# Attention steps of 512 and 234 columns instead of two halves of 373, in an audio tower on one core

## What is computed

```python
y = relu(patches @ W.T + b); h = batchnorm(y)                    # (16, 746, 128)
x = layernorm(h); q, k, v = heads(x @ Wq.T + bq), heads(x @ Wk.T + bk), heads(x @ Wv.T + bv)
probs = softmax(q @ k.T * 16 ** -0.5)                            # 8 heads, 746 x 746
h = h + merge(probs @ v) @ Wo.T + bo
x = layernorm(h); e = argmax(x @ Wr + br)                        # one expert a token; its gate is 1
h = h + relu(x @ W1[e] + b1[e]) @ W2[e] + b2[e]
```

## Time and profile before

| | |
|---|---|
| time, median of 3 runs (lowest to highest) | 1233.38 us (1231.71 to 1234.83) |
| span of the profiled execution | 1275.9 us; the profile gives no other time of its own |
| mean granted clock of TensorE | 0.965 |
| PE busy | 1178.7 us (92%) |
| DVE busy | 1072.5 us (84%) |
| ACT busy | 950.6 us (75%) |
| POOL busy | 680.0 us (53%) |
| load of a Q or K part, issue to landing (median) | 2.4 us |

### The profile page before, as it was taken

The page is one execution under the profiler, slowest core; times in us unless marked ns, Lnnn a source line. Parts: engine busy times, 40 slices in busy tenths (PEclk is TensorE's granted clock), DMA queues, the critical chain, the costliest instruction groups (busy, mean ns, idle before and its releaser), DMA issues.

```text
span 1275.9 us, 53879 instructions
## 1 busy us (share of the span) xinstructions
PE 1178.7 (92%) x21379; PEld 745.5 (58%) x21379; DVE 1072.5 (84%) x2756; ACT 950.6 (75%) x2477; POOL 680.0 (53%) x894
## 2 busy tenths in 40 slices
PE   6479999999999999999999999999999846899996
PEld 3334656555555556555555556565644326899996
DVE  7469899999999999999999999999999544577774
ACT  4426988888887878788888878797877824567774
POOL 2062436566473837475665739374723334456664
PEclk9768999999999999999999999999999969899998
DMA  8152132222313131323223131313220513333331
GB/s 190 39 84 79 40 86 72 76 84 61 94 52 94 45 105 42 104 72 79 83 63 93 51 94 45 106 41 104 72 80 28 150 56 105 88 93 105 103 101 50
DMA packets 79409, 102.32 MB, mean 80 GB/s; under 512 B 15916, under 2 KB 72995, under 8 KB 78734
## 3 DMA queue, kind: packets, MB, share of 16 engines
q1 hardware_dynamic: 70624, 79.02, 23.4%
q0 software_dynamic: 8384, 20.22, 5.1%
q10 hardware_dynamic: 186, 0.02, 0.0%
HBM read 60.76 MB, written 38.93 MB: 78 GB/s over the span
## 4 chain that ended last, share of the span: by engine, by line
PE 63%; DVE 20%; issue 5%; POOL 3%; ACT 2%; DMA 1%; SPq 1%; another core or an unknown queue 1%; POOLq 0%; DVEq 0%; ACTq 0%
PE psum L1247 36%; DVE half_max L1112 14%; PE psum L1312 13%; PE psum L1391 6%; PE psum L1401 5%; PE psum L1252 2%; ACT arena L808 2%; DVE stats L916 1%; POOL out_dram L720 1%; DVE rows L990 1%; PE psum L1382 1%; POOL arena L405 1%; DMA arena<-max_rows 1%; PE psum L1267 1%; DVE arena L962 1%
## 5 line engine op out<-in xcount | busy, mean ns | idle before, releaser
L1112 DVE TENSOR_REDUCE half_max<-psum 128x1 f32<-128x373 f32 x1536 | 760.8, 534 | 62.8 <-PE psum L1247 55.0
L808 ACT ACTIVATE arena<-psum 128x373 f32<-128x373 f32 (+1 forms) x1536 | 655.0, 489 | 154.4 <-PE psum L1247 139.0
L1247 PE MATMUL psum<-k_rows,arena 96*32 96x373 bf16 x6144 | 519.1, 329 | 14.9 <-DVE half_max L1112 6.1
L1247 PE MATMUL psum<-arena,k_rows 98*32 98x373 bf16 x6144 | 515.7, 326 | 13.7 <-ACT arena L808 6.2
L1312 PE MATMUL psum<-arena,values 128*32 128x373 f32 (+1 forms) x3072 | 313.2, 478 | 0.2
L1247 PEld LDWEIGHTS psum<-k_rows,arena 96*32 96x32 bf16 x6144 | 173.8, 96 | 195.7 <-DVE half_max L1112 103.4
L1247 PEld LDWEIGHTS psum<-arena,k_rows 98*32 98x32 bf16 x6144 | 176.4, 95 | 178.2 <-ACT arena L808 74.8
L631 POOL DMA_INDIRECT routed_rows_dram<-rows,pos_i x96 | 96.6, 1007 | 170.7 <-PE psum L1247 106.2
L720 POOL DMA_INDIRECT out_dram<-arena,slot_id x101 | 119.2, 1180 | 90.0 <-issue 51.5
L1312 PEld LDWEIGHTS psum<-arena,values 128*32 128x32 f32 (+1 forms) x3072 | 98.4, 110 | 20.7 <-issue 2.8
L861 ACT COPY arena<-psum 128x128 f32<-128x128 f32 x101 | 26.9, 266 | 77.7 <-PE psum L1382 39.7
(11 more groups left out here) (218 smaller groups left out, 1447.5 us busy)
## 6 DMA issues: line engine op xcount, KB each, us to landing
arena<-q_parts_dram SPq DMA_DIRECT2D x192, 93.2 KB, 2.4
k_rows<-k_parts_dram SPq DMA_DIRECT2D x192, 93.2 KB, 2.4
arena<-routed_rows_dram SPq DMA_DIRECT2D x101, 130.0 KB
q_parts_dram<-q_part SPq DMA_DIRECT2D x48, 186.5 KB, 2.3
k_parts_dram<-k_part SPq DMA_DIRECT2D x48, 186.5 KB, 2.0
arena<-in_x_t_dram SPq DMA_DIRECT2D x3, 703.1 KB, 14.1
seq<-in_w_dram SPq DMA_DIRECT2D x1, 2048.0 KB
seq<-in_w_dram SPq DMA_DIRECT2D x8, 256.0 KB
```

The costliest lines, as they stand in the source:

```text
L808: nc.scalar.activation(probs[0:kn(kt), G % N_P, j, :], st_bank[s % N_ST][0:kn(kt), 0:HALF], ACT.Exp).then_inc(s_exp, 1)
L1112: nc.vector.tensor_reduce(half_max[:, m:m + 1], mx_bank[m % N_MX][:, 0:HALF], AX.X, ALU.max)\
L1247: last = nc.tensor.matmul(dst[n:n + m], weights[:, n:n + m], moving, start=start, stop=stop)
```

## The change

The 746 queries of a score and the 746 keys of a maximum are cut at 512, so parts have 512 and 234 columns. A wide step is one head's 512; a narrow step takes the 234 of two heads, side by side in one bank (468 of 512 columns) and in one exponential or one reduction with two results. A body has 72 steps: for each four heads 24 wide ones and then 12 narrow ones. The maxima take turns: two heads' 512, then both heads' 234. A group that is weighed is one key tile and four heads, of 512 or of 234 queries, 24 groups a body as before; the six narrow groups lie in the memory of the three wide ones, and the step from which an exponential may overwrite a group is worked out in `weighed_before`. Each transpose `turn` waits for its own copy alone, where it waited for both. All step tables are set anew for 72 steps. The wider ring takes its memory from buffers that are laid over others (`by_tok`, `scored`, `mv`).

```diff
-    STEPS = H * 2 * NT
-    PASS = NT * GH
-    LEAD = 60
-    WEIGH_AT = (7, 11, 15, 19, 23, 27)
+    WIDE_Q = 512
+    NARROW_Q = L - WIDE_Q
+    WIDE_STEPS = NT * GH
+    HALF_STEPS = WIDE_STEPS + NT * GH // 2
+    STEPS = 2 * HALF_STEPS
+    LEAD = 48
+    WEIGH_AT = (7, 11, 15, 19, 24, 27, 31, 32, 34, 35, 37, 39)
...
+        narrow_probs = p_ring.rearrange("p (n t) -> p n t", n=NT)
...
         def step_of(s):
-            p, kt, j = s // PASS, s % PASS // GH, s % GH
-            return p // 2, p % 2, kt, GH * (p // 2) + j, j
+            g, r = s // HALF_STEPS, s % HALF_STEPS
+            if r < WIDE_STEPS:
+                return g, True, r // GH, r % GH
+            return g, False, (r - WIDE_STEPS) // 2, (r - WIDE_STEPS) % 2 * 2
...
+        def weighed_before(i, g, wide, kt):
+            first = i * GROUPS + g * HALF_GROUPS
+            if not wide:
+                return first + NT // 2 + kt // 2 + 1
+            return first + kt - 2 if kt >= N_P else first - NT + 2 * kt + 2
...
                         act.wait_ge(s_st, scores(i, s))
-                        nc.scalar.activation(probs[0:kn(kt), G % N_P, j, :], st_bank[s % N_ST][0:kn(kt), 0:HALF],
-                                             ACT.Exp).then_inc(s_exp, 1)
+                        if wide:
+                            nc.scalar.activation(probs[0:kn(kt), kt % N_P, j, :], st_bank[s % N_ST][0:kn(kt), 0:WIDE_Q],
+                                                 ACT.Exp).then_inc(s_exp, 1)
+                        else:
+                            nc.scalar.activation(narrow_probs[0:kn(kt), kt, NARROW_Q * j:NARROW_Q * (j + 2)],
+                                                 st_bank[s % N_ST][0:kn(kt), 0:2 * NARROW_Q],
+                                                 ACT.Exp).then_inc(s_exp, 1)
...
-                dve.wait_ge(s_o, r * 4 + 2 * (g + 1))
+                dve.wait_ge(s_o, r * 4 + 2 * g + 1 + k)
...
-                        nc.vector.tensor_reduce(half_max[:, m:m + 1], mx_bank[m % N_MX][:, 0:HALF], AX.X, ALU.max)\
-                          .then_inc(s_red, 1)
+                        n, part = m // 3, m % 3
+                        if part < 2:
+                            nc.vector.tensor_reduce(half_max[:, n, part:part + 1], mx_bank[m % N_MX][:, 0:WIDE_Q], AX.X, ALU.max)\
+                              .then_inc(s_red, 1)
+                        else:
+                            nc.vector.tensor_reduce(half_max[:, n, 2:4],
+                                                    mx_bank[m % N_MX][:, 0:2 * NARROW_Q].rearrange("p (a t) -> p a t", a=2),
+                                                    AX.X, ALU.max).then_inc(s_red, 1)
...
                 for j in range(GH):
...
+                    if wide:
+                        moving = probs[0:kn(kt), kt % N_P, j, :]
+                    else:
+                        moving = narrow_probs[0:kn(kt), kt, NARROW_Q * j:NARROW_Q * (j + 1)]
+                    last = nc.tensor.matmul(o_bank[32 * j:32 * (j + 1), 0:WIDE_Q if wide else NARROW_Q],
+                                            values[b % 3][0:kn(kt), kt, GH * g + j, :], moving,
+                                            start=kt == 0, stop=kt == NT - 1, skip_group_check=True)
```

More of the change, by code:

```diff
@@ L550, in body @@
                     if live(i, 0):
[L551 removed]
+                        sp.wait_ge(s_st, scores(i, HALF_STEPS - 1))
                     load_first_heads(i, par)
@@ L1298, in task, with weigh @@
                 last.then_inc(s_misc, 1)
-            def weigh(b, G, k):
-                p, kt = G // NT, G % NT
-                first = HALF * k // PARTS
-                n = HALF * (k + 1) // PARTS - first
-                if k == 0:
-                    pe.wait_ge(s_exp, scores(b, GH * (G + 1) - 1))
-                    if kt == 0:
-                        wait(pe, s_o, b * 4 + p)
-                for j in range(GH):
-                    last = nc.tensor.matmul(o_bank[32 * j:32 * (j + 1), first:first + n],
-                                            values[b % 3][0:kn(kt), kt, GH * (p // 2) + j, :],
-                                            probs[0:kn(kt), G % N_P, j, first:first + n],
-                                            start=kt == 0 and k == 0, stop=kt == NT - 1, skip_group_check=True)
-                if k == PARTS - 1:
-                    last.then_inc(s_pv, 1)
+            def weigh(b, G):
+                g, n = G // HALF_GROUPS, G % HALF_GROUPS
+                wide, kt = n < NT, n % NT
+                pe.wait_ge(s_exp, scores(b, last_step_of(G)))
+                if kt == 0:
+                    wait(pe, s_o, b * 4 + G // NT)
+                for j in range(GH):
+                    if wide:
[5 more added lines that the diff above has]
+                                            start=kt == 0, stop=kt == NT - 1, skip_group_check=True)
+                last.then_inc(s_pv, 1)
             def constants():
@@ L1354, in body @@
-                    for n, after in enumerate(WEIGH_AT):
-                        p = (s - after) // PASS
-                        if (s - after) % PASS == 0 and live(i, 0 if p >= 0 else -1):
-                            weigh(i if p >= 0 else i - 1, p % 4 * NT + n // PARTS, n % PARTS)
-                    if is_body(i, LAST_BODY) and s == WEIGH_AT[-1] - PASS + 1:
+                        if n < 2:
+                            quad(mx_bank[m % N_MX][:, 0:WIDE_Q], q_rows[b % 2][0:KR, 2 * u + n, D * t:D * (t + 1)],
+                                 k_rows[b % 2][0:KR, 2 * u + n, 0:WIDE_Q]).then_inc(s_mx, 1)
+                        else:
+                            for a in range(2):
+                                last = quad(mx_bank[m % N_MX][:, NARROW_Q * a:NARROW_Q * (a + 1)],
+                                            q_rows[b % 2][0:KR, 2 * u + a, D * t:D * (t + 1)],
+                                            k_rows[b % 2][0:KR, 2 * u + a, WIDE_Q:L])
+                            last.then_inc(s_mx, 1)
```

130 lines of the change are left out of this document (70 added, 60 removed).

## The result

| | before | after |
|---|---|---|
| time, median (lowest to highest) | 1233.55 us (1231.71 to 1234.83) | 1221.39 us (1220.99 to 1222.22) |
| after / before, 95% interval | | 0.9897 [0.9882, 0.9911] |
| span of the profiled execution | 1235.6 us in run 1 below | 1219.2 us |

The change saves 12.2 us, 1.0%, where the forecast was 28: the time lies 16 us above 1205 and just outside the forecast's own range of 1193 to 1220. The profiled execution of before that stands ahead of the prediction was 3.3% longer than the kernel's ordinary executions; comparisons here use a second profile of the same kernel, taken in run 1.

The account below looks back on a forecast made before the run. PE was taken as the bound, 55.2 us of work in a 58.6 us body. Half the 3.4 us stall over 15.4 bodies (26 us) plus 1.5 at the ends, 28 less than 1233.4, gave 1205 us, range 1193 to 1220.

Parts of the forecast that it names:

- The body takes 58.6, so PE stands still for about 3.4 us a body: Main loop before: a body of 58.6 us less 55.2 us of PE work leaves 3.4 us of PE stall.
- the term of 26 us: Main loop: half of PE's stall, 1.7 us a body, goes in 15.4 bodies, saving 26 us.
- The sentence in the sum that spreads the 3.3% over the bodies: Main loop: if the profile's extra 3.3% lies evenly, a body takes 56.7 us with 1.5 of stall, giving 1220 us.
- The other edits I cost at nothing: Shared buffers, bank of P rows and first loads: no added wait or instruction, 0 us.
- PE's work: TensorE in one body: 55.2 us of work, the same before and after the change.
- DVE's relief: Maxima on VectorE: 72 reductions instead of 96, of 0.598 and 0.552 us, take 1.5 us of load off a body.
- Narrow quads do not wait for weights: Judges a rival on TensorE: narrow quads wait for weights at 0.107 us, 7.5 us back, 1212 us; chance 0.10.
- The waits behind the residual and for the maxima's DMA: Main loop: MAX1's wait behind the residual, 0.4 us a body, and most of the DMA wait, some 0.5, go.
- All stalls gone: Rival, main loop: DVE has 1.8 us of room and PE never waits, 54 us less, 1180 us; chance 0.11.
- Slower by fillers that wait for ACT: Rival, main loop: five fillers each wait one exponential of 0.6 us, 18 us more, 1252 us; chance 0.08.
- The hand-over: Rival, PE and DVE: hand-over, not load, makes the stalls; at most 0.3 us a body goes, 1228 us; chance 0.13.
- The ends: Start and end outside the joint part, maxima alone and last scores alone: together about -1.5 us.

Follow-up runs that it names:

- run 1: The kernel before, unchanged, profiled a second time: 1237.45 us in a single execution.
- run 6: The kernel before, with every reduction reading 187 of its 373 columns: 1216.23 us, 0.9836 of before.
- run 12: The changed kernel with rank product, joint maxima's difference and MAX0 at later steps, and their rounded copy made by a second reduction: 1206.20 us, 0.9766 of before.
- run 7: The changed kernel, with every reduction reading half of its columns (256 of 512, 117 of each 234): 1188.20 us, 0.9612 of before.
- run 8: The kernel before, with the rank product and the two operations behind it at steps 86, 88, 90 instead of 82, 87, 89: 1232.42 us, 0.9961 of before.

## Why the prediction was wrong, step by step

- **The step that failed first: "The body takes 58.6, so PE stands still for about 3.4 us a body".** The 58.6 came from an execution that was longer than the runs. There PE's late starts do add up to 3.6 us a body; in run 1, where a body takes 56.70, they are 1.9, and making DVE light brings back 0.9 (run 6). So the term of 26 us, half of 3.4 in 15.4 bodies, would have been some 15 with 1.9. The sentence in the sum that spreads the 3.3% over the bodies had the right base (56.7 us, "1220"); the forecast should have stood on it.
- **The step that failed second: "The other edits I cost at nothing".** New tables move small DVE operations past POOL's list. That cost 15.2 us (after against run 12), and the late starts did not shrink at all (1.9 us a body in run 1, 2.2 in after). The prediction asked of a moved step who is queued behind it and whether PE has made its input, not what POOL is doing at that moment.
- **PE's work, put the same on both sides, was right; 55.2 us was a little high.** A body less its late starts behind quads is 54.3 to 54.8 us in runs 1, 6, 7, 12 and after.
- **Run 12 stands at 1206, the forecast at 1205; that is luck.** Its bodies gain 56.70 - 55.44 = 1.26 us where the forecast had 1.7, and the ends gain more than the 1.5 us that it gave them (below). That half of the stall goes did come out: 1.94 us of late starts became 1.01.
- **DVE's relief was right.** In the part with maxima alone, the chain of after has 0.60 us for each of two wide reductions and 0.55 for a narrow one, against 0.598 and 0.552:

```profile
83.61 0.55 DVE half_max L1138
84.16 1.20 DVE half_max L1135 x2
```

  A body's DVE time went from 54.3 us (run 8) to 52.5 (run 12), both without collisions: 1.8 us against 1.5. The 125 ns of the Trainium skill ("Perfetto Trace Analysis", Optimizing Scalar/DVE Operations), by which it would have been 3.0 (an estimate), are not what these reductions show.
- **Narrow quads do not wait for weights.** Two start within 0.20 us, four wide ones within 0.88 (timeline of PE, run 7). The 0.107 us a quad that the prediction worked out from the Trainium skill ("TensorE: Matmul & The Clock Gate", LDWEIGHTS) are not seen:

```profile
640.35 0.41 PE L1274 MATMUL psum<-arena,k_rows 98*32 98x234 bf16 x8
640.55 0.41 PE L1274 MATMUL psum<-k_rows,arena 96*32 96x234 bf16 x8
...
641.81 0.42 PE L1274 MATMUL psum<-arena,k_rows 98*32 98x512 bf16 x4
...
642.69 0.59 PE L1339 MATMUL psum<-arena,values 128*32 128x234 f32 x8
```

- **The waits behind the residual and for the maxima's DMA went, as said.** MAX1's wait of the earlier trace rows has no row in after, and the DMA's 15.7 us in 32 waits became 0.8 in 2. Counted by late starts in run 1, the residual was worth 0.3 us a body (0.4 in the prediction), the DMA only 0.1 (some 0.5). The new wait of DVE for the ranks at step 57 appears once in the whole span, in the last body, and costs the loop nothing.
- **The other rivals.** All stalls gone, 1180 us: that takes a DVE that cannot be late, and then it is 1188 (run 7). Slower by fillers that wait for ACT: PE's gaps end with DVE, not with ACT's copies. The hand-over, 1228: run 12 stands far below it; after itself, at 1221, is nearer to it than to 1205, but because of the collisions.
- **The ends were sized too small:** -1.5 us predicted, 12.8 measured (run 1, where the first maximum starts at 72.4 us and the last score at 1000.6: 928.2 - 680.4 = 247.8; after: 235.0). The row of the first stretch of scores, and the last half body with maxima and the scores without them, in run 1:

```profile
103.40:109.60 6.20, 6.18 (x76) 2.99 (x80) 4.87 (x10) 3.85 (x8) 0.00 (x0) 0.52 0.70 189
...
946.40:973.00 26.60, 25.94 (x527) 13.58 (x523) 26.08 (x62) 20.62 (x51) 6.42 (x7) 1.00 0.10 33
973.00:1000.60 27.60, 22.42 (x393) 8.97 (x386) 8.51 (x45) 24.29 (x62) 13.87 (x25) 1.00 0.68 189
```

  and in after:

```profile
102.00:108.00 6.00, 6.00 (x126) 2.79 (x119) 4.89 (x9) 5.04 (x11) 0.00 (x0) 0.94 0.56 138
...
934.20:959.00 24.80, 24.77 (x534) 14.53 (x530) 24.80 (x51) 19.40 (x39) 6.13 (x7) 1.00 0.10 34
959.00:985.10 26.10, 23.57 (x454) 10.32 (x450) 8.99 (x46) 24.40 (x52) 13.38 (x24) 1.00 0.72 197
```

  Where fillers are missing, DVE is busy without a gap (24.80 of 24.80): the last half body loses 1.8 us, 1.3 of them DVE's busy time. The body before loses 1.6, the second body 1.3. The scores alone take 26.1 us for 48 steps, within the predicted 26 to 29, and 1.5 less than the 60 steps before. The larger lead takes the predicted 2.4 us, the maxima alone take 1.0 less instead of 0.8 more, which is not clear of the difference between executions (31.0 to 32.4 us in before, run 1 and run 8). The last 3.2 us are the first scores, in the next section.

## What to carry to other kernels

Make the sum against the time of the runs before any stall is counted: a stall is a small difference of two large numbers, and an execution 3% too long doubled it here (3.6 us a body against 1.9). When a step table moves, set each moved DVE operation beside what POOL runs at that moment: here a copy or a product that started behind POOL's subtraction of two SBUF tensors lasted as long as that did, and a reduction could stand in for the copy. To learn what an engine's lateness is worth, make that engine light and read the body, and then read by starts whose waits come in its place: in run 6 those of ACT and POOL, which busy times hide.

## What the hardware showed that was not expected

A DVE product of 48 elements took 0.20 us alone and 1.52 behind POOL's subtraction of two SBUF operands. POOL's scaling of rows (L407, one tensor read) did not do that: a routing product of the same size, also of two SBUF operands, started 0.62 to 0.71 us into one that lasted 0.82, in 14 bodies, and took its usual time (shortest/median/longest ns over the span):

```profile
L1030 DVE TENSOR_TENSOR scored<-scored,rank_e x16: 191/196/209, 191.2 to 998.4; 128x48 f32<-128x48 f32 x16
```

So not every POOL operation that reads SBUF held DVE up, as far as POOL's rough times can tell; the rule of the Trainium skill cited above is wider than that.

The other surprise was the granted clock of the first scores. In run 1 it was 0.52 for 6 us, nearly all of it the lower level of 1.2 GHz. In after it was 0.94, and in run 8, the kernel before but for three steps of small operations:

```profile
104.00:110.20 6.20, 6.20 (x139) 3.13 (x143) 5.39 (x13) 4.73 (x13) 0.00 (x0) 1.00 0.70 186
```

In all three PE had done maxima alone before it, waiting for DVE between quads. At 0.52 the stretch costs an estimated 3 us (6.2 x 0.48); in run 8 the way from the first score to the third join is 2.6 us shorter than in run 1. These come and go between executions and can't be put down to the change.
